# Stage borders of a four-layer network on one core: mixture weights, returned rows, root table, first operands, identity, z products and small scales

## The reference

```
xn = layernorm(x)
x = x + attn_L(xn) + ffn_L(xn)          # L = 0, 1, 2, 3
```

## Time and profile before

| what | value |
|---|---|
| median of three runs | 992.84 us |
| the profiled execution itself | 993.59 us |
| its span | 991.8 us |
| TensorE matmuls busy | 873.3 us (88%) |
| VectorE busy | 803.1 us (81%) |
| ScalarE busy | 606.5 us (61%) |
| GpSimd busy | 200.2 us (20%) |
| mean granted TensorE clock | 0.929 |

### The profile page before, as it was taken

How to read it: one execution, slowest core, us unless ns; L and a number is a source line. 1 busy time by engine, 2 the same in 40 slices (tenths; PEclk the granted TensorE clock), 3 DMA queues, 4 the chain that set the end, 5 groups by cost and what they waited for, 6 DMA issues and landing times. The chain is left out here.

```text
span 991.8 us, 22162 instructions
## 1 busy us (share of the span) xinstructions
PE 873.3 (88%) x8501; PEld 448.1 (45%) x8501; DVE 803.1 (81%) x1600; ACT 606.5 (61%) x1312; POOL 200.2 (20%) x249
## 2 busy tenths in 40 slices
PE   5689999999999998893779999999998988786888
PEld 3312222222222222892434545554546666565578
DVE  7798999999999990555689888889864777799687
ACT  3318888888888887452416777777772447232652
POOL 2301132521312120451110011102010031233132
PEclk9659999999999999896859999999998998988899
DMA  2541535454156421111364674345301000000001
GB/s 72 167 127 46 140 79 123 91 107 97 47 121 144 124 61 22 48 34 56 68 195 119 170 155 97 82 99 112 74 8 36 1 1 1 1 1 0 4 7 37
DMA packets 61782, 73.72 MB, mean 74 GB/s; under 512 B 20247, under 2 KB 45968, under 8 KB 61662
## 3 DMA queue, kind: packets, MB, share of 16 engines
q1 hardware_dynamic: 47354, 49.22, 20.7%
q0 software_dynamic: 8576, 17.86, 7.4%
q10 hardware_dynamic: 5748, 5.22, 1.6%
HBM read 44.59 MB, written 18.16 MB: 63 GB/s over the span
## 5 line engine op out<-in xcount | busy, mean ns | idle before, releaser
L1035 DVE TENSOR_REDUCE a_negmax<-a_mbank 128x1 f32<-128x1024 f32 (+4 forms) x640 | 491.4, 819 | 40.5 <-PE a_mbank L828 18.7
L990 ACT ACTIVATE a_probs<-a_ebank 128x512 f32<-128x512 f32 (+3 forms) x896 | 426.3, 559 | 104.3 <-PE a_ebank L856 52.3
L828 PE MATMUL a_mbank<-a_moving,a_still 48*128 48x512 bf16 (+4 forms) x1280 | 274.7, 377 | 23.2 <-DVE a_ident L997 14.1
L856 PE MATMUL a_ebank<-b_moving,b_still 50*128 50x512 bf16 (+4 forms) x1280 | 249.5, 356 | 9.6 <-ACT a_probs L990 7.3
L881 PE MATMUL a_acc<-a_probs,a_slot_v 128*32 128x512 f32 (+3 forms) x1792 | 216.8, 560 | 0.8 <-ACT a_probs L990 0.7
L856 PEld LDWEIGHTS a_ebank<-b_moving,b_still 58*64 58x64 bf16 (+1 forms) x1280 | 83.1, 101 | 200.9 <-ACT a_probs L990 167.2
L828 PEld LDWEIGHTS a_mbank<-a_moving,a_still 56*64 56x64 bf16 (+1 forms) x1280 | 70.1, 102 | 122.4 <-DVE a_negmax L1035 94.0
L865 PE MATMUL a_ebank<-a_bias_b,anti 64*64 64x176 bf16 (+4 forms) x1728 | 77.9, 226 | 0.0
L865 PEld LDWEIGHTS a_ebank<-a_bias_b,anti 64*64 64x64 bf16 x1728 | 64.7, 107 | 4.7
L836 PE MATMUL a_mbank<-bias_a,anti 64*64 64x176 bf16 (+2 forms) x576 | 66.2, 236 | 0.0
L881 PEld LDWEIGHTS a_acc<-a_probs,a_slot_v 128*32 128x32 f32 x1792 | 36.4, 108 | 53.6 <-issue 36.1
(11 more groups left out here) (389 smaller groups left out, 1114.0 us busy)
## 6 DMA issues: line engine op xcount, KB each, us to landing
a_slot_v<-vo SPq DMA_DIRECT2D x16, 512.0 KB
b_moving<-stack SPq DMA_DIRECT2D x64, 96.0 KB
b_still<-stack SPq DMA_DIRECT2D x32, 192.0 KB
a_still<-stack SPq DMA_DIRECT2D x60, 96.0 KB, 2.9
a_moving<-stack SPq DMA_DIRECT2D x60, 96.0 KB, 3.0
expert<-in_expert_rows POOLq DMA_DIRECT2D x8, 578.0 KB, 4.1
a_bias_b<-trow SPq DMA_DIRECT2D x32, 66.0 KB
stack<-expert SPq DMA_DIRECT2D x4, 384.0 KB, 2.8
```

The lines of the kernel that those rows point to most:

```text
L828: last = nc.tensor.matmul(mbank[COLS * c:COLS * (c + 1), bank, lo - left:hi - left], S.a_still[rows, q % 2, pr, at[c]:at[c] + COLS], S.a_m ...
L856: last = nc.tensor.matmul(ebank[COLS * c:COLS * (c + 1), step % NE, lo:512], S.b_still[rows, buf, pr, at:at + COLS], S.b_moving[rows, buf, ...
L990: nc.scalar.activation(probs[:, (q * G + g) % NPB, j, lows[g]:512], ebank[:, step % NE, lows[g]:512], ACT.Exp).then_inc(p_full, 1)
L1035: nc.vector.tensor_reduce(to[:, at:at + 1], mbank[:, (index - 1) % NM, 0:right - left], AX.X, ALU.max, negate=True).then_inc(m_empty, 1)
```

## The change

Eight edits, and nothing else:

1. `front_phase`, layer 1 only: ScalarE loads the table of the root before it waits for anything.
2. `front_phase`, layer 1 only: pair 0 of the first operands is loaded by SyncE, pair 1 by ScalarE after its last cast. GpSimd issues neither. Layer 0 stays as it was.
3. `attention_phase`, both layers: the bf16 identity is made by ScalarE, ahead of its table load.
4. `experts_and_projection`: quarters 0 and 2 of the returned rows by SyncE, 1 and 3 by ScalarE.
5. `moe_phase`: the store of wT and the load of wE by GpSimd, at the head of its list, instead of SyncE at the end of its own.
6. `fp4_scale` takes 1e-12 as an immediate instead of a tile; `fp4_nudge` drops the minimum with its input (same value for the positive scales). Both become tensor_scalar.
7. `third_phase`: GpSimd computes z * g + offset for all four chunks in one row.
8. `third_phase`: GpSimd adds to S.x two tiles at a time, as their two moves are done, and `add` waits every second tile.

```diff
@@ front_phase @@
+            if not first:
+                nc.scalar.preload_act_table(ACT.Sqrt)
             act.wait_ge(eps_set, 1)
...
             middle(2 * CHUNKS - 1)
+            if not first:
+                act.wait_ge(S.first_stored, 2 * 96)
+                for jj in range(2):
+                    for dma in load_first_pass(act, S, True, 0, 1, jj):
+                        dma.then_inc(S.first_loaded[1], 16)
...
-            pool.wait_ge(S.first_stored, 2 * 96)
-            for jj in range(2):
-                for dma in load_first_pass(pool, S, not first, 0, 0, jj):
-                    dma.then_inc(S.first_loaded[0], 16)
+            if first:
+                pool.wait_ge(S.first_stored, 2 * 96)
+                for jj in range(2):
+                    for dma in load_first_pass(pool, S, False, 0, 0, jj):
+                        dma.then_inc(S.first_loaded[0], 16)
...
+            pr = 1 if first else 0
             for jj in range(2):
-                for dma in load_first_pass(sp, S, not first, 0, 1, jj):
-                    dma.then_inc(S.first_loaded[1], 16)
+                for dma in load_first_pass(sp, S, not first, 0, pr, jj):
+                    dma.then_inc(S.first_loaded[pr], 16)
@@ attention_phase @@
+            nc.scalar.copy(ident[:], S.ident[:]).then_inc(ident_ready, 1)
             nc.scalar.preload_act_table(ACT.Exp)
...
-            nc.vector.tensor_copy(ident[:], S.ident[:]).then_inc(ident_ready, 1)
@@ experts_and_projection @@
+        def bring_back(eng, quarters):
+            for i in range(YB):
+                eng.wait_ge(sent[i], 16 * ((NB - 1 - i) // YB + 1))
+            for i in quarters:
+                part = slice(i * NT // 4, (i + 1) * NT // 4)
+                eng.dma_start(back[:, part, :],
+                              S.spread_dram[0:TOK].rearrange("(t p) c -> p t c", p=P)[:, part, :]
+                              ).then_inc(returned[i], 16)
...
             act.wait_ge(h_done, NB)
+            bring_back(act, (1, 3))
...
+            bring_back(sp, (0, 2))
@@ moe_phase @@
+            pool.wait_ge(wT_ready, 1)
+            pool.dma_start(S.w_dram.rearrange("e (t p) -> t e p", p=P), wT[:]).then_inc(w_stored, 16)
+            pool.wait_ge(w_stored, 16)
+            pool.dma_start(wE[:], S.w_dram).then_inc(wE_loaded, 16)
             pool.wait_ge(inverses_loaded, 16 * QUAD)
...
-            sp.wait_ge(wT_ready, 1)
-            sp.dma_start(S.w_dram.rearrange("e (t p) -> t e p", p=P), wT[:]).then_inc(w_stored, 16)
-            sp.wait_ge(w_stored, 16)
-            sp.dma_start(wE[:], S.w_dram).then_inc(wE_loaded, 16)
@@ fp4_scale, fp4_nudge @@
-    return V.scalar_tensor_tensor(big, big, 1.0 / 6.0, tiny[:, 0:1].to_broadcast([P, big.shape[1]]), ALU.mult, ALU.max)
+    return V.tensor_scalar(big, big, 1.0 / 6.0, 1e-12, ALU.mult, ALU.max)
-    return V.scalar_tensor_tensor(inv, inv, 1.0 - 2.0 ** -22, inv, ALU.mult, ALU.min)
+    return V.tensor_scalar(inv, inv, 1.0 - 2.0 ** -22, None, ALU.mult)
@@ third_phase @@
             for c in range(CHUNKS):
                 s = slice(CT * c, CT * (c + 1))
                 nc.gpsimd.tensor_tensor(zg[:, s], z[:, s], spread(S.row3[:, 0, :]), ALU.mult).then_inc(side, 1)
-                pool.wait_ge(side, 3 * c + 2)
+                pool.wait_ge(side, 2 * c + 2)
                 nc.gpsimd.tensor_tensor(zg[:, s], zg[:, s], spread(offset[:]), ALU.add).then_inc(side, 1)
-                pool.wait_ge(side, 3 * c + 3)
-                pool.wait_ge(moved, CT * (c + 1))
-                nc.gpsimd.tensor_tensor(S.x[:, s], S.x[:, s], zg[:, s], ALU.add).then_inc(side, 1)
+            for t in range(0, NT, 2):
+                pool.wait_ge(side, 2 * (t // CT + 1) + 1)
+                pool.wait_ge(moved, t + 2)
+                nc.gpsimd.tensor_tensor(S.x[:, t:t + 2, :], S.x[:, t:t + 2, :], zg[:, t:t + 2, :], ALU.add
+                                        ).then_inc(joined, 1)
...
-                if t % CT == 0:
-                    dve.wait_ge(side, 3 * (t // CT) + 4)
+                if t % 2 == 0:
+                    dve.wait_ge(joined, t // 2 + 1)
```

More of the change, by code:

```diff
@@ L2148, in third_phase @@
                              "gated_ready", "p_full", "added", "written"))
+        joined = sem("joined")
         turns = [("z", 0), ("z", 1), ("z", 2), ("k", 0), ("z", 3), ("k", 1), ("k", 2), ("k", 3)]
@@ L2333, in _ @@
             pool.wait_ge(side, 1)
+            spread = lambda a: a.unsqueeze(1).to_broadcast([P, CT, P])
             for c in range(CHUNKS):
                 s = slice(CT * c, CT * (c + 1))
-                spread = lambda a: a.unsqueeze(1).to_broadcast([P, CT, P])
                 nc.gpsimd.tensor_tensor(zg[:, s], z[:, s], spread(S.row3[:, 0, :]), ALU.mult).then_inc(side, 1)
-                pool.wait_ge(side, 3 * c + 2)
+                pool.wait_ge(side, 2 * c + 2)
                 nc.gpsimd.tensor_tensor(zg[:, s], zg[:, s], spread(offset[:]), ALU.add).then_inc(side, 1)
-                pool.wait_ge(side, 3 * c + 3)
-                pool.wait_ge(moved, CT * (c + 1))
-                nc.gpsimd.tensor_tensor(S.x[:, s], S.x[:, s], zg[:, s], ALU.add).then_inc(side, 1)
+            for t in range(0, NT, 2):
[3 more added lines that the diff above has]
+                                        ).then_inc(joined, 1)
         @block.vector
```

## The result

The changed kernel takes 980.33 us (median of 4 runs, 978.73 to 982.99) against 993.13 for the kernel before: the ratio is 0.9871, 95% interval 0.9834 to 0.9908. A second series of six runs gave 980.54. The forecast was 983.0 with a range of 978.5 to 988. The profiled execution is the longest of the first four: 982.99 us, span 981.2.

A forecast was written before the change was run, and what follows sets the result against it. TensorE, nine tenths busy or more in most attention slices, has no slack, so border gains carry through. Terms 0.3 + 0.5 + 2.7 + 5.4 + 0.3 + 0.7 = 9.9 off 993.59 or 992.84 gave 983 us, range 978.5 to 988.

The forecast's parts named there:

- A: Causal attention's border: the stores don't hold TensorE, the border gives up to 5.7 us, 980 in all; chance 0.15.
- B: Last stage: scalings wait for whole GpSimd instructions, five times up to 1.29 us; stage loses 3.8, 987.5 in all; chance 0.15.
- E: Border with layer 1: its gain doesn't come, ScalarE's issues being as late as the drain; 985.7 us; chance 0.1.
- C: Mixture stage: weights still late, GpSimd's queue costing more than SyncE's; landing at 760.5 gives 988.4 us; chance 0.06.
- Rows back on two queues: End of layer 0's experts: ScalarE issuing two quarters shortens the third's wait; 0.3 us gained, bounds 0 and 0.91.
- Early root table: Layer 1's front: table loaded at stage start removes VectorE's wait for the root; 0.5 us gained (0 to 0.54).
- First operands and identity: Causal attention's start: earlier stage and first matmul, partly lost behind ScalarE's stores; 2.7 us gained, bounds 0 and 5.7.
- Mixture weights: Mixture stage, first chunk: TensorE's second bias starts at 757.8 without waiting for wE; 5.4 us gained, bounds 0 and 5.4.
- The legs: Mixture weights' arrival, priced by SyncE's rows: store to landing 5.8 us, load to use 2.5, 3 to spare.
- D: Mixture weights later than C: the change loses from a landing at 765.0 on; at 771, 999 us; chance 0.03.
- Scales with immediates: Thirteen quantisations, nine of the first kind in layer 2: shorter small VectorE instructions; 0.3 us gained, bounds 0 and 1.6.
- Z ahead: Last stage: TensorE's amat wait shrinks, 2.6 us; input projection loses 1.9; net gain 0.7, from 2.9 gained to 5.1 lost.

The follow-up runs named there:

- the kernel that takes the wait away: Changed kernel with the causal attention's two semaphore increments ahead of ScalarE's twelve stores; 979.29 us, ratio 0.986.
- the pieces of 0.5 us: Changed kernel with increments ahead of ScalarE's stores and GpSimd's z work in 32 instructions of 128 columns instead of 8 of 512; 980.56 us, ratio 0.9878.
- the early increments: Changed kernel with the causal attention's two increments ahead of ScalarE's stores, alone (979.29 us) or with further edits (fastest 977.44).

## Why the prediction was right, point by point

The time came out 2.7 us under the forecast, inside the range. The sum was made on the time of the profiled execution; there it is 982.99 against 983.7. The medians fell by 12.8 us in the first series and by 10.9 in the second (991.4 to 980.54), the profiled executions by 10.6, and the forecast was 9.9: up to 2.2 us of the first series are not read from any row. The chances for a time under 989.9 add up to 0.96 in the prediction's own list (0.51, A, B, E and most of C), not to 0.92.

- **Rows back on two queues**, 0.3 taken: 0. The end of the additions lies 8.98 to 9.44 us after the last scatter's issue in the nine traces with two queues (mean 9.20), 8.63 to 9.11 in the five with one (mean 8.87). The share of 1.06 was the row to go by, and its bound of zero the value. The row that misled me is the 0.91 us wait for the third quarter: it fell to 0.26, and the first quarter came 1.0 later, with all four now issued within 1.0 us. The wait was also partly that execution's: in the kernel with only the weights moved, whose code is the same there, it is 0.19 (and 0.53 ahead of the second quarter). The Trainium skill, page "DMA: Bandwidth & Descriptors", section "Issuing engines are not separate DMA queues", says that issuing from several engines saves no more than the issue time; the traces agree, and here even the 1.0 us saved at the issues was not seen at the end.
- **Early root table**, 0.5: 0.62.
- **First operands and identity**, 2.7: 2.8 at the first exponential in the profiled execution, 3.3 in the mean of five. The step by step working holds: against the logits' addition, the stage starts 1.97 earlier (2.07 by the kernel that gives the operands back; 1.6 forecast, and ScalarE's issues end at 491.7, the last 0.46 us long), first matmul 0.36 after it, TensorE standing 4.3 (3.3 forecast, 3.3 in the second trace). The stores' scatter of 1 us is as large as the difference, so that the total came out to 0.1 is luck. Rival A is refuted by the name of the releaser, L969, and by the kernel that takes the wait away. I had not said that 0.5 of the lead goes again by the last exponential.
- **Mixture weights**, 5.4: 5.46, and up to 0.3 more by the start of layer 2, which the forecast put at nothing. The legs were mis-sized to the safe side: from the store's issue to the load's 2.64 us by GpSimd, not 5.8. The nearest row had nine other copies of its queue ahead of it. Rivals C and D were never near.
- **Scales with immediates**, 0.3: 0.34 by their own durations. The 0.45 over layer 2 is no test: the same code took 104.05 and 105.42 us there in two traces.
- **Z ahead**, 0.7 net (2.6 gained, 1.9 lost): 1.6 (3.1, 1.5). The places of gain and loss are those of the forecast; the gain was sized 0.5 too small and the loss 0.4 too large. How a meeting works was rival B's part, and its whole-instruction waits are what the trace shows, not the mean of 0.53 us that the forecast took from L1958: the scaling from 923.65 ends 0.28 us after GpSimd's instruction from 923.41 does, and three others likewise. Its price was wrong: four were met, not five, and waited 0.95 each; of these 3.8 us only 1.5 reached the end of the projection. The forecast's 1.9 was near that by luck: five meetings of 0.53 us, where four cost 0.95 each. The Trainium skill, page "SBUF — State Buffer", section "SBUF: two separate sides", states that VectorE and GpSimd share a pair of ports to SBUF, which an instruction of one holds to its end against the other; the traces agree, down to the pieces of 0.5 us, which cost a scaling 0.25 at most. The gain was larger than forecast (3.1, not 2.6), and VectorE's own instructions, no longer beside GpSimd's, got shorter: the sixteen results amat take 5.1 us instead of 8.7. How that makes the extra 0.5 was not followed further.
- **What the sum left out** is the clock: +1.46 in layer 0, -1.60 at the mixture stage, both of the execution. That they cancel here is luck; in another execution either can be smaller or missing, and six of fourteen traces had the slow start.

Open: the medians of the kernels with one part undone lie 3 to 5.5 us above the changed kernel's, 2 to 4 more than their traces lose at the edits. Four runs each, spread over 2.4 to 5.6 us, can't settle it. The profiled execution was the shortest of its four in three of these five kernels and the longest in the changed kernel, so traces alone rank them otherwise than medians do: the kernel with GpSimd's issues back has a span of 980.9, the changed kernel 981.2 and 979.3. The size of each part therefore rests on the stretches of the traces, not on the times. Whether the falls of the clock in layer 1 come more often with the early increments (three of five traces, none of nine without) was not separated from chance either.

## What to carry to other kernels

A wait that is taken away shows what stands behind it: list each wait of the waiting engine up to the next shared semaphore, and move increments that depend on nothing ahead of long lists of issues (3.4 us at the place here, about 1 us on the medians). Give a small transfer on the critical path to an idle engine's queue rather than behind others on the usual one; a second queue for large copies that already fill the DMA engines gives nothing. When GpSimd work is moved beside VectorE work on SBUF, cut it into pieces as short as the delay that VectorE can bear.

## What the hardware showed

- The same kernel starts its mixture stage at clock 0.51 in one execution and 1.00 in another, after the same 1.96 us of TensorE's idle time; it costs 1.4 to 1.6 us. TensorE fell at this border in the kernels with spans of 984.2, 981.2, 977.7, 978.9, 980.9 and 975.7, and not in the other eight.
- From the start of the causal attention the clock stays at 0.50 for 19 to 26 us; it rose at 521.0 before, at 515.5 in the changed kernel and at 512.1 with the early increments. In the eight traces in which TensorE does not stand before the turn it is 0.93 to 0.94 busy from its first matmul to this rise, and still it stays low for 18.6 to 21.5 us. In the six in which it stands there the rise comes 22.4 to 23.8 us after the stage's start, in the five with the early increments 18.9 to 19.4: the stand-still removed gave back clock as well.
- ScalarE's twelve stores took 11.5 to 13.3 us in fourteen traces, 12.56 and 11.48 in two of the same kernel: 1 us of scatter in the turn of the maxima from this queue alone.
- A VectorE scaling of 0.54 us that met a GpSimd instruction of 1.3 to 1.5 us ended 0.28 to 0.29 us after that one did, all four times in the changed kernel's trace.
